# Projections of two attention layers: v of each token group behind its q and k, in place of one stretch between the halves

## The reference

```python
x = x + attn_a(layernorm(x))
x = x + ffn(layernorm(x))
x = x + attn_b(layernorm(x))
x = x + ffn(layernorm(x))
# in attention:
q, k, v = split_heads(x @ Wq.T), split_heads(x @ Wk.T), split_heads(x @ Wv.T)
# in ffn: logits of every token against phi_w, 2048 rows of 256, with phi_b
```

## Time and profile before

| | us |
|---|---|
| median of three runs | 4777.9 (4777.64 to 4795.27) |
| profiled execution | 4784.3 |
| its span | 4782.5 |
| projections of layer a: first VectorE work to the next phase's first matmul | 20.39 to 139.57 |
| projections of layer b: the same | 2410.72 to 2518.11 |

### The profile page before, as it was taken

The page is one execution under the profiler, slowest core; times in us unless marked ns, Lnnn a source line. Parts: engine busy times, 40 slices in busy tenths (PEclk is TensorE's granted clock), DMA queues, the critical chain, the costliest instruction groups (busy, mean ns, idle before and its releaser), DMA issues. The chain is left out here.

```text
span 4782.5 us, 97694 instructions
## 1 busy us (share of the span) xinstructions
PE 4441.6 (93%) x40558; PEld 1955.9 (41%) x40558; DVE 4075.7 (85%) x4651; ACT 3132.5 (65%) x5879; POOL 1211.5 (25%) x1201
## 2 busy tenths in 40 slices
PE   7799999999998899899997999999999998998998
PEld 4222223222224566456662222232222345664666
DVE  5899998999885898678848999989998868885887
ACT  3378988889997444334344789888899974443443
POOL 1100001100002576445301000011000015774543
PEclk9799999999999899999997999999999999999999
DMA  6100000000000000310040000000000000004000
GB/s 183 54 21 2 2 15 15 14 14 4 2 2 23 1 1 1 107 36 0 0 126 26 17 2 2 22 9 15 15 2 2 2 22 1 1 1 142 10 13 13
DMA packets 73767, 112.29 MB, mean 23 GB/s; under 512 B 12501, under 2 KB 56789, under 8 KB 69077
## 3 DMA queue, kind: packets, MB, share of 16 engines
q1 hardware_dynamic: 68746, 99.96, 6.3%
q0 software_dynamic: 4608, 6.50, 1.0%
HBM read 73.70 MB, written 31.47 MB: 22 GB/s over the span
## 5 line engine op out<-in xcount | busy, mean ns | idle before, releaser
L889 DVE TENSOR_REDUCE b_att_mx<-ps 128x2 f32<-128x1024 f32 (+3 forms) x1152 | 1228.4, 1130 | 105.9 <-PE ps L742 80.6
L889 DVE TENSOR_REDUCE a_att_mx<-ps 128x2 f32<-128x1024 f32 (+3 forms) x1152 | 1227.9, 1130 | 102.3 <-PE ps L742 77.7
L846 ACT ACTIVATE b_att_pt<-ps 128x512 f32<-128x512 f32 (+3 forms) x2304 | 1146.9, 560 | 208.7 <-PE ps L778 179.0
L846 ACT ACTIVATE a_att_pt<-ps 128x512 f32<-128x512 f32 (+3 forms) x2304 | 1146.9, 560 | 207.2 <-PE ps L778 177.3
L797 PE MATMUL ps<-b_att_pt,b_v 128*17 128x256 f32 (+1 forms) x8704 | 672.6, 381 | 10.7 <-ACT b_att_osb L833 9.8
L797 PE MATMUL ps<-a_att_pt,a_v 128*17 128x256 f32 (+1 forms) x8704 | 670.5, 380 | 10.7 <-ACT a_att_osb L833 9.7
L723 POOL TENSOR_SCALAR_AFFINE_SELECT b_att_pt<-b_att_pt 128x512 f32<-128x512 f32 x128 | 81.4, 636 | 1122.9 <-ACT b_att_pt L846 1110.6
L723 POOL TENSOR_SCALAR_AFFINE_SELECT a_att_pt<-a_att_pt 128x512 f32<-128x512 f32 x128 | 81.4, 636 | 1120.4 <-ACT a_att_pt L846 1108.1
L778 PE MATMUL ps<-b_q,b_k 51*128 51x512 f16 (+3 forms) x1152 | 363.2, 370 | 0.2 <-ACT b_att_pt L846 0.2
L778 PE MATMUL ps<-a_q,a_k 51*128 51x512 f16 (+3 forms) x1152 | 361.3, 368 | 0.2 <-ACT a_att_pt L846 0.2
L742 PE MATMUL ps<-a_k,a_q 48*128 48x512 f16 (+3 forms) x1152 | 293.9, 379 | 51.9 <-DVE a_att_mx L889 37.9
(11 more groups left out here) (319 smaller groups left out, 7241.0 us busy)
## 6 DMA issues: line engine op xcount, KB each, us to landing
f_mix_ct<-in_expert_w SPq DMA_DIRECT2D x64, 256.0 KB, 4.2
g_mix_ct<-in_expert_w SPq DMA_DIRECT2D x64, 256.0 KB, 4.3
a_parts_q<-a_qkv_cut SPq DMA_DIRECT2D x24, 256.0 KB
a_parts_k<-a_qkv_cut SPq DMA_DIRECT2D x24, 256.0 KB
b_parts_q<-b_qkv_cut SPq DMA_DIRECT2D x24, 256.0 KB
b_parts_k<-b_qkv_cut SPq DMA_DIRECT2D x24, 256.0 KB
x<-in_x SPq DMA_DIRECT2D x8, 512.0 KB, 8.6
out<-x SPq DMA_DIRECT2D x8, 512.0 KB, 2.9
```

What stands on the lines that cost most here:

```text
L846: act.activation(pt[:, s % PT_RING, i, 0:width], ps[:, at:at + width], ACT.Exp, scale=unscale).then_inc(pt_ready, 1)
L889: dve.tensor_reduce(mx[u % 2][:, h:h + 2, t, c], both, AX.X, ALU.max).then_inc(ring_read, 1)
```

## The change

`values` gets a group g and makes the four tiles of that group alone. It is called behind the two first-half blocks of each group. v uses banks 6 and 7 in turn (4 to 7 before), so a tile waits for the copy of the tile two ahead of it (four before). ScalarE's copies of v move to the same place, behind the highs of the group.

```diff
-            def values():
+            def values(g):
                 pe.wait_ge(w_loaded[2], 16)
-                for t in range(T):
-                    wait(pe, v_kept, t - 3)
+                for t in range(KB * g, KB * (g + 1)):
+                    wait(pe, v_kept, t - 1)
                     for c in range(DC):
-                        mm = pe.matmul(ps[:, (4 + t % 4) * BANK:(4 + t % 4) * BANK + D], xlnT[:, c, t * P:(t + 1) * P],
+                        mm = pe.matmul(ps[:, (6 + t % 2) * BANK:(6 + t % 2) * BANK + D], xlnT[:, c, t * P:(t + 1) * P],
                                        w[2][:, c, :], start=(c == 0), stop=(c == DC - 1))
                     mm.then_inc(v_made, 1)
...
                 project(2 * g)
                 project(2 * g + 1)
-            values()
+                values(g)
             for n in range(BLOCKS, 2 * BLOCKS):
                 project(n)
...
                 make_high(2 * g)
                 make_high(2 * g + 1)
-            for t in range(T):
-                act.wait_ge(v_made, t + 1)
-                act.activation(v[:, t, :, 0:HD], ps[:, (4 + t % 4) * BANK:(4 + t % 4) * BANK + D].rearrange("p (h d) -> p h d", d=HD),
-                               ACT.Copy).then_inc(v_kept, 1)
+                for t in range(KB * g, KB * (g + 1)):
+                    act.wait_ge(v_made, t + 1)
+                    act.activation(v[:, t, :, 0:HD], ps[:, (6 + t % 2) * BANK:(6 + t % 2) * BANK + D].rearrange("p (h d) -> p h d", d=HD),
+                                   ACT.Copy).then_inc(v_kept, 1)
             for n in range(BLOCKS, 2 * BLOCKS):
                 make_high(n)
```

## The result

The changed kernel takes 4809.8 us (median of five runs, 4809.17 to 4823.78) against 4777.9 (again the median, now of five): ratio 1.006, interval 1.0047 to 1.0074. It is slower by some 30 us, as forecast (4811.9). The profiled execution takes 4809.17 us (span 4807.4), 24.9 more than the profiled one of before, which stood 6.4 above its own median.

What follows compares the result with a forecast made beforehand. TensorE was busy 4441.6 of 4782.5 us, with VectorE nearly full too in the projections' first half. Layer a +23.0 and layer b +11.0 made +34 us on the 4777.9 median: 4811.9 us, range 4798 to 4828.

Steps and rivals of the forecast that it cites:

- v ahead of F: First half of both layers' projections: seven groups' v, 24.2 us, less 1.2 us of waits, moves F by +23.0 us per layer.
- F: The instant when the low of block 15 ends on VectorE: 67.92 in layer a, 2457.75 in b, before the change.
- The 1.2 us of tile waits: First half: TensorE's waits for VectorE's normalised tiles over five periods, expected to go with a period of 7.75 us.
- The two banks: v in two banks instead of four: taken as 0 us, at most 6 us per layer if the release is slower.
- Layer a keeps its 71.7 us behind F: Layer a: the fold, then stores held by head loads, keep the next phase at F + 71.7; the layer loses 23.0 us.
- at F + 48.8 again: Layer a, ScalarE: block 24 starts as far behind F as before, its stores held by the same head loads.
- The bounds I gave: Layer a: 6.5 us less (+16.5) if head loads ran as fast as b's; 2 us more for the clock.
- The new meeting in b: Layer b, second half: stores meet head loads, block 24 goes at F + 31 against F + 17.5 wanted; the layer loses 11.0 us.
- Rival 1: Layer b's stores pass the head loads unhindered, so only layer a loses: +21.8 us, 4799.7; chance 0.12.
- Rival 2: Layer b's head loads turn slow like a's: +51.8 us, 4829.7; chance 0.12.
- Rival 3: Layer a's head loads turn fast: +27.5 us, 4805.4; chance 0.07.
- Rival 4: First half: TensorE had hidden room for v, so F stays: a +0, b -12 us, 4765.9; chance 0.03.

## Why the prediction was right

The forecast stood on three terms.

- **v ahead of F: +23.0 us per layer.** Measured 23.4 in a and 23.2 in b. The 1.2 us of tile waits went (the period is 7.76 us against the 7.75 forecast), but a little more was spent at the start (the first two blocks take 5.59 us in a, 5.18 before, and 4.88 in b, 4.69 before; why, no row shows). The two banks cost nothing, by the changed profile and by the run of their own.
- **Layer a keeps its 71.7 us behind F: +23.0 in all.** The mechanism is as forecast: TensorE stood 22.61 us against 21.4, until the fold was done (the wait ended with the fold's own last step, L102, and not with a low behind it, at the same instant within 0.2 us), and behind it the stores of job 8 were held by the head loads, which set block 24. The profile shows + 19.2 because what follows F happened to be 4 us shorter; with layer a changed alone the whole cost 25 us by its ratio, and the phase 142.3 - 119.2 = 23.1. The step that block 24 goes "at F + 48.8 again" holds in the mean: 47.3 over three runs in the old order (44.7 to 48.8), 47.4 over two in the new (45.1 and 49.7). The bounds I gave, 6.5 us less and 2 more, had other reasons than this spread, and the runs before already lay 17.6 us apart, half of the figure I was after. One size was off without effect: by my steps the fold alone would have set block 24 at F + 40.8; without loads beside it, it is F + 38.6.
- **The new meeting in b: +11.0 us.** Measured + 9.1 in the profile, 10 by the ratio of b alone. Block 24 goes at F + 27.5 where F + 17.5 is wanted: the stores cost it 10.0 us, 13.5 by my steps. The mis-sized term is the loads' hold on the stores: I took every store packet of job 8 to wait for one load packet on every engine, or for the end of the loads. Neither is what the rows show. From 2507 to 2515 one store packet moved, where one for one there would have been over a hundred; from 2515 on, with the loads at 76.8% of the engines and less, the stores went beside them, long before the loads ended at F + 36.2. From block 24 to the last low it took 13.1 us in place of 12.1 (k stores were late once more, 3.62 us), and TensorE ran its last four blocks in 10.03 us, at first at a granted clock of 0.50 (2528 to 2530), as forecast.

That 4809.8 lies within 2.1 us of 4811.9 is in part luck. The two terms together were 34 us; the two phases show 28.3, the ratio 29 (22 to 35), and the medians 31.9, with a median of before that came out at 4780.9 to 4784.5 on later occasions.

In a, the wait changed its place in a way I had said in words but not priced: in today's order phi, fold and head loads all lie beneath v, so none of them shows in the profile of before except by the 7.99 us. Taking v away uncovers both, and of the two the fold (F + 38.6) lies below the loads (F + 45 to 50): the 22.61 us for which TensorE stands are the longest wait in its row, but they are not what the layer's length hangs on.

Rival 1 (b's stores slip through) falls with the 11.09 us. Rival 2 falls with head packets of 0.892 x 128 / 133 = 0.86 us in b (2507 to 2515; 1.09 MB are 133 packets of 8 KB), where it wanted over 1. Rival 3 (a's loads turn fast) gave 4805.4, not far from the 4809.8, and the whole alone would not refute it; but block 24 of a was to go at F + 41 and went at 45.1 and 49.7, and the loads stayed slow. Rival 4 falls with the period of 7.76 us. The cause of layer a's slow loads, on which rivals 2 and 3 hung, is told below.

The Trainium skill ("DMA: Bandwidth & Descriptors", Queues, rings and completion order) says that an engine takes turns between queues a packet at a time, and that such a packet is typically 9 to 17 descriptors. Turns between single packets of the profile, as I had read it, are not what this trace shows: the one store packet in 8 us speaks against them, and so do the 16.0 us of a's job 8, which I took to agree: 24 x (1.21 + 0.09) would be 31 us. Turns between such bundles would fit; as an estimate from the page's figure, 9 to 17 times 0.86 us are 8 to 15 us for the loads' turn. That a packet of the profile is one descriptor no run here shows. The run with short rows is what either reading wants (half the packet length, the same bytes, and the wait is down to TensorE's own 1.09 us), but its slower issue would do the same.

## What to carry to other kernels

A stretch of one engine between two halves may be what hides the other work that hangs on the first half's end: before spreading it out, list what is released at that end (a transfer, a fold, loads from another queue) and what then lies bare. Work without deadlines, as v here, is worth most where nothing else can run: beneath the fold and behind the last block, while stores land. The longest wait on the timeline need not be the last limit: here a second one ended later and moved along. And loads with long rows on one queue delayed stores with short rows on another far beyond their share of the bytes; cutting the loads into four times as many with rows of the same length as the stores' removed it in b.

## What I had not expected

The head loads of layer a were slow (1.21 us a packet, 0.80 in b), and I had left the cause open. With phi behind job 3 the fold still lies beside the loads, from 105 to 109:

```profile
q0 software_dynamic: 75, 0.61, 102.6%
```

That is 1.026 x 64 / 75 = 0.88 us a packet, b's speed. With phi in its old place (layer a changed alone, 104 to 108) it is 0.951 x 64 / 42 = 1.45 us:

```profile
q0 software_dynamic: 42, 0.34, 95.1%
```

So not VectorE's fold beside the loads makes them slow, but the 2048 KB transfer of phi that is still under way when they start, and they stay slow for some 20 us after it has landed. The kernel before says the same of the fold: from 78 to 82, ahead of it, VectorE is busy for 0.00 us, and the loads already fill 102.2% of the engines for 0.37 MB. With the loads behind all stores the same shows once more: in a, where the result of the fold (2 x 1024 KB) is being stored as they are issued, the next phase starts 43.4 us behind the first load (57.4 to 100.8 behind F), in b 32.0 us. Why they don't recover is open; it was not tried.
